# A two-layer mixture-of-experts block: the first layer's experts half dense and half sorted by expert through memory, with the order laid out anew

## The chip, the cores and the metric

The program runs on one core of a Trainium2 chip. The time is the device time of one launch in microseconds; a result is the median of several runs. The core has a matrix engine (PE), a vector engine (DVE), an activation engine (ACT), a general engine (POOL, GpSimd) and a queue engine (SP) that here only issues transfers. Each runs its own list of instructions in order; they meet through counting semaphores. PE writes only to eight accumulation banks (`bank`), which DVE and ACT empty.

## What is computed

4 batches of 512 tokens, 256 features each, go through two layers. Cut to what matters:

```
h0  = einsum('bnt,bot->bno', x, sum_g y[b,g] * weight[g] * mask) + bias        # layer 0 input
p   = softmax(h0 @ router_w.T); top 2 of 8 experts, weights normalised
x  += sum over the token's 2 experts of (h0 @ W_e + p_e) * w_e                  # 8 experts, 256 x 256
h1  = x @ W_base.T + b + 2 * sum_e w[b,e] * (x @ A_e.T) @ B_e.T                 # layer 1 input
x  += sum over 2 shared experts of swiglu(h1)                                   # F = 352 each
x  += sum over the token's 2 of 8 experts of w_e * swiglu_e(h1)
```

Every large product is made of float16 halves (high and low part) in three passes, to keep float32 accuracy.

## The kernel before

The 2048 tokens are 16 tiles of 128 rows (four per batch). `hs` holds the layer input with the feature on the partitions, `x1` the running result with the token on the partitions.

**Layer 0, dense.** All eight experts are applied to all 16 tiles. The loop `for m in range(TWO)` (PE L1100, DVE L761, ACT L538) takes two tiles at a time; inside, `j` runs over four pairs of experts. Per tile and pair PE makes six matmuls of 512 columns, and DVE adds the two experts' halves of the bank into `x1`, each with its own coefficient (zero for experts not chosen): L777, 128 instructions in all. Behind it on the same engines come, tile pair by tile pair, the turning of `x1` (`transposes`, `tr_hi`, `tr_lo`), the low-rank weights (`lora`, `wl_sum`, `wl_hi`), the layer 1 input of a batch (`layer1_input`, `h_hi`, `h_lo`), its router logits, and the token rows for the later gather (`token_rows`, `copy_rows`, bank 4 or 5 in turn). The layer 1 weights come in 16 pieces: SP loads a piece, ACT makes the high half and the scaled copy (L529, L532), POOL subtracts to the low half in eight shares (L442).

**Layer 1, shared experts.** A round `i` is a batch and one of six strips of F. PE: `gate_up(i)`, twelve matmuls of 512 columns (six in every sixth round). ACT: silu (`sil`). DVE: product (`prod`). ACT: high half (`acts`). DVE: low half. `gate_up(i)` may start when `prod(i-2)` is made. Rounds 0 to 17 (`EARLY`) run ahead of the routed tiles; within them stand `down(0)` behind round 7 and `down(1)` behind round 17, 68 matmuls of 256 columns each. DVE also does the bookkeeping of the routing between rounds: the choice of two experts (after round 2), the group sizes and slots (rounds 4 and 5), one-hot rows (`hot_lanes` within the emptying of `down(0)`, `hot_tiles` in rounds 8 to 10), `slot_tokens` (12) and the table of each tile's expert (`tile_experts`, 14), which PE loads into registers before round 17.

**Layer 1, routed experts.** 39 tiles of 128 sorted entries: POOL gathers rows by an indirect transfer, PE turns and multiplies, POOL scatters the result to memory (`results`). The gate and up products of tile i, the transposes of tile i+2 and the down product of tile i-1 are interleaved (`step`).

**The tail.** Rounds 18 to 23, `down(2)`, `down(3)`; SP loads the scattered rows back (`yg`), ACT scales the first expert's rows, POOL adds them, DVE adds the second (`combine`), then DVE adds the shared part (`accumulate`) and SP stores.

## Time and profile before

| | |
|---|---|
| median of 3 runs | 379.43 us (377.74 to 380.24) |
| profiled execution, device time | 378.77 us |
| its span, first to last instruction | 377.0 us |
| PE busy | 357.7 us, 95% of the span |
| DVE busy | 238.8 us, 63% |
| ACT busy | 166.1 us, 44% |
| POOL busy | 154.2 us, 41% |
| mean granted TensorE clock | 0.994 |

A matmul row's duration is the time through the array, which overlaps with the next; the pace of a train is its length over its count. Idle time of an engine is put down to whatever released it last.

### The profile page before, as it was taken

The page shows a single profiled execution, that of the slowest core. Times are in us where ns is not written, and L with a number is a line of the kernel's source. Part 1 is how long each engine was busy: PE and PEld are TensorE (multiplying, and loading weights), DVE is VectorE, ACT ScalarE, POOL GpSimd, SP SyncE. Part 2 cuts the span into 40 slices and gives each one's busy share as a digit, 9 for nine tenths or more (in the row PEclk, how much of TensorE's full clock was granted, in tenths as well). Part 3 has the DMA queues.
Part 4 walks back from the last instruction along what each step waited for, and adds up shares of the span by engine and source line. Part 5 has one row for each costly group of instructions (what it writes and reads, how often), then busy time and mean ns, then how long its engine had stood idle before and what let it go on. Part 6 is the DMA issues. An engine that isn't in the chain of part 4 may idle for free.

```text
span 377.0 us, 7974 instructions
## 1 busy us (share of the span) xinstructions
PE 357.7 (95%) x2713; PEld 225.4 (60%) x2714; DVE 238.8 (63%) x594; ACT 166.1 (44%) x286; POOL 154.2 (41%) x241
## 2 busy tenths in 40 slices
PE   7998999999999999989999999999999999999992
PEld 3543544455454454555447677777777777776561
DVE  1357999676766646778775455565555565546476
ACT  1045376567555765543442333333333333323560
POOL 3000564665647532000020365565665555532642
PEclk9999999999999999999999999999999999999997
DMA  7985113433443420100000122222222222212942
GB/s 217 377 330 203 54 53 119 150 92 122 141 151 128 136 69 0 58 0 2 0 28 2 44 86 84 70 84 78 75 83 80 73 78 78 80 42 74 353 161 111
DMA packets 18038, 39.26 MB, mean 104 GB/s; under 512 B 2976, under 2 KB 9376, under 8 KB 17888
## 3 DMA queue, kind: packets, MB, share of 16 engines
q1 hardware_dynamic: 13552, 28.71, 22.8%
q0 software_dynamic: 3744, 10.23, 8.7%
q8 instruction: 14, 0.23, 0.3%
q10 hardware_dynamic: 720, 0.02, 0.1%
q14 instruction: 8, 0.07, 0.1%
HBM read 29.65 MB, written 9.31 MB: 103 GB/s over the span
## 4 chain that ended last, share of the span: by engine, by line
PE 72%; DVE 16%; DMA 4%; ACT 3%; issue 3%; SPq 0%; DVEq 0%
PE bank L1000 58%; PE bank L1147 4%; PE bank L1245 3%; DVE prod L904 2%; PE bank L1016 2%; PE bank L1229 2%; ACT acts L582 2%; DVE x L892 2%; DMA w1s<-results 2%; DVE x L777 2%; DVE acts L910 1%; DMA x<-wc 1%; PE bank L1076 1%; DMA results<-yb,row_out 1%; ACT sil L572 1%
## 5 line engine op out<-in xcount | busy, mean ns | idle before, releaser
L442 POOL TENSOR_TENSOR w1s<-piece,w1s 128x170 f16<-128x170 f32 x128 | 61.6, 521 | 78.2 <-ACT piece L532 78.2
L1000 PE MATMUL bank<-w0s,hs 128*128 128x512 f16 x384 | 86.0, 379 | 1.2 <-DVE x L777 1.2
L1000 PE MATMUL bank<-w1s,rT 128*128 x468 | 76.2, 313 | 1.6 <-DVE rT L964 1.6
L451 POOL DMA_INDIRECT rows<-token_store,row_in x39 | 37.9, 971 | 86.1 <-DVE row_in L874 47.5
L777 DVE SCALAR_TENSOR_TENSOR x<-bank,coef,x 128x256 f32<-128x256 f32 x128 | 54.8, 478 | 19.4 <-PE bank L1000 19.1
L1000 PEld LDWEIGHTS bank<-w0s,hs 128*128 128x128 f16 x384 | 36.9, 98 | 43.8 <-DVE x L777 1.9
L1000 PE MATMUL bank<-hs,w1s 128*128 128x512 f16 x264 | 59.6, 379 | 2.1 <-DVE prod L904 2.1
L1000 PEld LDWEIGHTS bank<-w1s,rT 128*128 128x128 f16 x468 | 44.0, 98 | 22.1 <-issue 2.1
L456 POOL DMA_INDIRECT results<-yb,row_out x39 | 38.5, 987 | 37.1 <-ACT yb L606 37.1
L1000 PE MATMUL bank<-w1s,aT 128*128 (+1 forms) x351 | 44.8, 273 | 0.8 <-DVE aT L957 0.8
L600 ACT ACTIVATE ract<-prod 128x352 f16<-128x352 f32 x39 | 19.4, 497 | 58.5 <-DVE prod L970 33.6
L1000 PEld LDWEIGHTS bank<-hs,w1s 128*128 128x128 f16 x264 | 25.0, 98 | 32.3 <-DVE prod L904 5.2
L964 DVE COPY rT<-bank 128x256 f32<-128x256 f32 x39 | 16.6, 425 | 33.3 <-PE bank L1229 33.3
L1000 PEld LDWEIGHTS bank<-w1s,aT 128*128 128x128 f16 (+1 forms) x351 | 32.7, 98 | 4.5 <-issue 0.9
L973 DVE TENSOR_TENSOR ract<-prod,ract 128x352 f16<-128x352 f32 x39 | 20.5, 526 | 21.9 <-issue 18.5
L1147 PE MATMUL bank<-w1s,acts 128*128 128x256 f16 x272 | 30.5, 273 | 1.5 <-DVE slot_lo L839 1.2
L595 ACT ACTIVATE sil<-bank 128x352 f32<-128x352 f32 x39 | 18.1, 463 | 28.5 <-PE bank L1000 28.5
L1147 PEld LDWEIGHTS bank<-w1s,acts 128*128 128x128 f16 x272 | 26.4, 98 | 6.1 <-issue 1.7
L582 ACT ACTIVATE acts<-prod 128x512 f16<-128x512 f32 (+1 forms) x24 | 15.1, 629 | 30.7 <-DVE prod L904 30.7
L529 ACT ACTIVATE w1s<-piece 128x1360 f16<-128x1360 f32 x16 | 21.3, 1329 | 14.7 <-DMA piece<-w 14.7
L910 DVE TENSOR_TENSOR acts<-prod,acts 128x512 f16<-128x512 f32 (+1 forms) x24 | 16.7, 697 | 16.0 <-ACT acts L582 16.0
L532 ACT ACTIVATE piece<-piece 128x1360 f32<-128x1360 f32 x16 | 21.4, 1338 | 0.5
(149 smaller groups left out, 405.5 us busy)
## 6 DMA issues: line engine op xcount, KB each, us to landing
piece<-w SPq DMA_DIRECT2D x16, 680.0 KB, 3.9
w1s<-results SPq DMA_DIRECT2D x6, 512.0 KB, 8.3
x<-wc SPq DMA_DIRECT2D x4, 512.0 KB, 7.0
w1s<-xT SPq DMA_DIRECT2D x4, 512.0 KB, 11.0
w1s<-w SPq DMA_DIRECT2D x4, 512.0 KB, 10.1
token_store<-xrow SPq DMA_DIRECT2D x4, 512.0 KB, 3.3
out<-x SPq DMA_DIRECT2D x8, 256.0 KB, 2.2
x<-x SPq DMA_DIRECT2D x1, 1536.0 KB, 11.7
```

Of the source, the lines that this page charges most:

```text
L442: ins = nc.gpsimd.tensor_tensor(w1s[:, LO, at], piece[:, i % 2, part], w1s[:, HI, at], ALU.subtract)
L451: pool.indirect_dma_start(rows[:, i % 2], None, token_store, bass.IndirectOffsetOnAxis(row_in[:, i:i + 1], 0)).then_inc(s_row[i % 2], 16)
L456: pool.indirect_dma_start(results, bass.IndirectOffsetOnAxis(row_out[:, i:i + 1], 0), yb[:, i % 2], None).then_inc(s_put[i % 2], 16)
L529: nc.scalar.activation(w1s[:, HI, i * PIECE:(i + 1) * PIECE], piece[:, i % 2], ACT.Copy, scale=SW).then_inc(sm["s_pchi"], 1)
L532: nc.scalar.activation(piece[:, i % 2], piece[:, i % 2], ACT.Copy, scale=SW).then_inc(sm["s_pcsc"], 1)
L582: nc.scalar.activation(acts[0:M, c % 2, f, HI], prod[0:M, p], ACT.Copy).then_inc(sm["s_ahi"], 1)
L600: nc.scalar.activation(ract[:, q, HI], prod[:, q, 0:F], ACT.Copy).then_inc(sm["s_rhi"], 1)
L777: nc.vector.scalar_tensor_tensor(x1[:, t], bank[(n + a) % 4][:, h * D:(h + 1) * D], coef[:, t, e:e + 1], x1[:, t], ALU.mult, ALU.add).then ...
L910: nc.vector.tensor_tensor(low, prod[0:M, p], acts[0:M, c % 2, f, HI], ALU.subtract).then_inc(sm["s_alo"], 1)
L973: nc.vector.tensor_tensor(ract[:, q, LO], prod[:, q, 0:F], ract[:, q, HI], ALU.subtract).then_inc(sm["s_rlo"], 1)
L1000: mm = nc.tensor.matmul(out_ap, l, r, start=(i == 0), stop=(i == len(terms) - 1))
L1147: mm = nc.tensor.matmul(bank[4 + q][:, 0:D], acts[:, c % 2, f, a, q * P:(q + 1) * P], w_dn(b, f), start=(f == 0 and n == 0), stop=(f == ST ...
```

## The change

Layer 0's experts stay dense for the first 8 tiles (batches 0 and 1). For the other 8 (`NTR`, batches 2 and 3) every token's two entries are sorted by expert into 23 tiles of 128 slots (`TILES0`):

- POOL scatters each token row to its two slots in memory (`place`, 16 indirect transfers); the slots were set to zero before (`clear`). SP loads the 23 slot tiles (`load_rows0`, four deep), PE turns each (`operand_rows`, 4 transposes), DVE copies it to `rT0` (`operand0`), PE multiplies it with its one expert (`sorted_tile`, 6 matmuls of 256 columns), ACT empties the bank (`out0`), SP stores it (`keep_out0`), POOL gathers both entries of each token (`take`, 16 indirect transfers), and DVE adds them with their weights (`combine0`, 32 instructions).
- This needs its own choice, ranks and slots before (`selected`, `ranks(rank0, ...)`, `slots0`, `parts0`, `tile_experts0`) and token rows of layer 0's input (`rows_of_layer0`, 32 transposes; `copy_rows0`).
- The tiles stand in bursts of four behind the rounds 2 to 7 of the shared experts.
- `EARLY` is 21 instead of 18. `down(0)` and `down(1)` stand both behind round 11, in halves, between the turning of the four late tile pairs and the layer 1 input of batches 2 and 3. The bookkeeping of layer 1's routing moves to rounds 9 and 12 to 19.
- Weight pieces are converted in another sequence (`ORDER`); the last six come behind the sorted tiles, since `w0s`, the slot rows and the gathered rows lie in the same memory.

The core of the diff:

```diff
-    EARLY = 3 * ST
-    DOWN = {ST + 1: 0, EARLY - 1: 1, EARLY + 1: 2}
+    EARLY = 3 * ST + 3
+    DOWN = {EARLY + 1: 2}
-    SCALED = {EARLY + 1: (0, 1), EARLY + 3: (2,), B * ST - 1: (3,)}
+    SCALED = {EARLY + 1: (0, 1), B * ST - 1: (2, 3)}
...
@@ POOL
+            for n in range(4):
+                low_parts(n)
+            pool.wait_ge(sm["s_slots0"], 1)
+            pool.wait_ge(sm["s_zero"], 16 * 2)
+            for t in range(NTR):
+                for k in range(K_TOP):
+                    place(t, k)
+                    i = t * K_TOP + k
+                    low_part(4 + i // SHARES, i % SHARES)
...
@@ ACT
                 if m == 1:
+                    copy_rows0(range(NTD, NTD + TPB))
                     act.wait_ge(s_x1[1], 16)
                     act.wait_ge(sm["s_r0"], 2)
...
+                if i in (8, 10):
+                    piece_hi(FREE - 4 + i // 2)
+                if i in (9, 11):
+                    piece_scaled(FREE - 4 + i // 2)
+                if i == 10:
+                    exps(2, DENSE, 1.0 / (SH1 * SW))
...
@@ DVE
+                if i == 9:
+                    dve.wait_ge(sm["s_m0"], TILES0)
+                    take_logits(1, 0, DENSE)
+                    largest(DENSE)
+                    second(DENSE)
+                    selected(DENSE, "s_sel")
+                if i == 11:
+                    combine0(8)
+                    tr_lo(4)
+                    accumulate(0, (), (0, 1))
+                    combine0(10)
...
@@ PE
-            for m in range(TWO):
+            for m in range(TWO_D):
...
+                    if m == 1:
+                        rows_of_layer0(range(NTD + 2 * j, NTD + 2 * j + 2))
...
+                for t in burst(i):
+                    sorted_tile(t, places0[t % BURST])
+                    if t + 2 < TILES0:
+                        operand_rows(t + 2)
+                if i == 11:
+                    transposes(4)
+                    down(0, quarters=(0, 1))
+                    transposes(5)
+                    down(0, quarters=(2, 3))
+                    layer1_input(2)
+                    transposes(6)
+                    down(1, quarters=(0, 1))
+                    transposes(7)
+                    down(1, quarters=(2, 3))
+                    layer1_input(3)
```

`transposes(4)` waits for `combine0(8)`:

```diff
+                else:
+                    pe.wait_ge(sm["s_cmb0"], (m - TWO_D + 1) * 2 * K_TOP)
+                    pe.wait_ge(sm["s_prod"], ND * ST - 1 + (m - TWO_D) // 2)
```

How the order moves. PE before, from the turning of the token rows of the last batch to the first expert table (`ident,hs` are token rows, `hs,w1s` of 12 a round's gate and up, `w1s,acts` a down, `wls,yg` the inverse of the sorting):

```order
L1087 MATMUL bank<-ident,hs 128x128 x8
L1174 MATMUL bank<-sel,before 128x128
L1176 MATMUL bank<-sel,ones 128x128 x15
L1179 MATMUL bank<-sel,ones 128x8 x16
L1000 MATMUL bank<-hs,w1s 128x512 x30
L1147 MATMUL bank<-w1s,acts 128x256 x68
```

PE of the change, rounds 10 and 11 (one train of 18) and what stands behind them (`ident,x` turns a tile pair of `x1`, `xrow,wls` is the layer 1 input of a batch):

```order
L1286 MATMUL bank<-hs,w1s 128x512 x18
L1365 MATMUL bank<-ident,x 128x128 x4
L1470 MATMUL bank<-w1s,acts 128x256 x34
L1365 MATMUL bank<-ident,x 128x128 x4
L1470 MATMUL bank<-w1s,acts 128x256 x34
L1286 MATMUL bank<-xrow,wls 128x512 x12
L1365 MATMUL bank<-ident,x 128x128 x4
L1470 MATMUL bank<-w1s,acts 128x256 x34
L1365 MATMUL bank<-ident,x 128x128 x4
L1470 MATMUL bank<-w1s,acts 128x256 x34
L1286 MATMUL bank<-xrow,wls 128x512 x12
L1286 MATMUL bank<-hs,w1s 128x512 x12
```

Before, a whole down stood behind seven rounds with bookkeeping; now both downs stand ahead of round 12, cut in halves, each half behind a turning of tiles.

ACT of the change from round 10 to the first late tile pair (the two table loads stand around the exponential; `w1s<-piece` and `piece<-piece` are a weight piece, `xrow<-bank` the turned tile pair):

```order
L740 ACTIVATE sil<-bank 128x512
L752 ACTIVATE acts<-prod 128x512
L674 ACTIVATE w1s<-piece 128x1360
L642 ACT_TABLE_LOAD
L642 ACTIVATE ex<-ex 128x64
L642 ACT_TABLE_LOAD
L740 ACTIVATE sil<-bank 64x512
L752 ACTIVATE acts<-prod 64x512
L679 ACTIVATE piece<-piece 128x1360
L660 ACTIVATE xrow<-bank 128x2x256
```

The silu of round 11 stands behind a piece's high half and the exponential with its tables.

DVE before, from the slots behind round 5 to the first quarter of `down(0)` (`yg<-lane` are the one-hot rows, eight at a time; `x<-bank,x` empties a quarter of `down(0)`):

```order
L839 SCALAR_TENSOR_TENSOR slot_lo<-slot_hi,st 128x32
L904 SCALAR_TENSOR_TENSOR prod<-bank,sil 128x512
L910 TENSOR_TENSOR acts<-prod,acts 128x512
L904 SCALAR_TENSOR_TENSOR prod<-bank,sil 128x512
L910 TENSOR_TENSOR acts<-prod,acts 128x512
L848 TENSOR_SCALAR yg<-lane,slot_lo 128x128 x8
L922 SCALAR_TENSOR_TENSOR x<-bank,x 128x256
```

DVE of the change, rounds 15 to 18 (the slots stand ahead of it, in round 14):

```order
L1055 TENSOR_SCALAR yg<-lane,slot_lo 128x128 x16
L1115 SCALAR_TENSOR_TENSOR prod<-bank,sil 128x512
L1123 TENSOR_TENSOR acts<-prod,acts 128x512
L1055 TENSOR_SCALAR yg<-lane,slot_lo 128x128 x16
L1115 SCALAR_TENSOR_TENSOR prod<-bank,sil 64x512
L1123 TENSOR_TENSOR acts<-prod,acts 64x512
L1061 TENSOR_TENSOR wls<-tile,slot_hi 128x32x39
L1064 TENSOR_SCALAR wls<-wls,lane 128x32x39
L1066 TENSOR_TENSOR wls<-wls,order 128x32x39
L1115 SCALAR_TENSOR_TENSOR prod<-bank,sil 128x512
```

The one-hot work stands between rounds now, with no down on PE beside it.

## Rows read from the trace of the kernel before

**Rows 1.** The page, busy time of each engine over the span.

```profile
PE 357.7 (95%) x2713; PEld 225.4 (60%) x2714; DVE 238.8 (63%) x594; ACT 166.1 (44%) x286; POOL 154.2 (41%) x241
```

**Rows 2.** The chain that ended last: start us, us, what (x matmuls).

```profile
91.08 12.95 PE bank L1000 x60
...
164.92 7.58 PE bank L1147 x68
```

**Rows 3.** The timeline, PE: start us, us, line, operation, count.

```profile
150.65 0.61 PE L1087 MATMUL bank<-ident,hs 128*128 128x128 f16 x8
151.09 2.75 PE L1000 MATMUL bank<-hs,w1s 128*128 128x512 f16 x12
```

**Rows 4.** The timeline, round 2 of the shared experts: silu, product, low half.

```profile
147.65 0.60 ACT L572 ACTIVATE sil<-bank 128x512 f32<-128x512 f32 x1 [1.39 <-PE bank L1000]
...
148.28 0.69 DVE L904 SCALAR_TENSOR_TENSOR prod<-bank,sil 128x512 f32<-128x512 f32 x1 [0.95 <-ACT sil L572]
...
149.67 0.69 DVE L910 TENSOR_TENSOR acts<-prod,acts 128x512 f16<-128x512 f32 x1 [0.70 <-ACT acts L582]
```

**Rows 5.** Busy time by window, DVE: window, its length, busy us (count with edges), clock, DMA.

```profile
56.51:59.41 2.90, 2.56 (x11) 1.00 0.53 169
150.28:154.92 4.64, 4.19 (x17) 1.00 0.00 0
162.32:164.77 2.45, 2.17 (x9) 1.00 0.00 0
168.79:170.18 1.39, 1.39 (x10) 1.00 0.00 0
177.76:179.21 1.45, 1.45 (x2) 1.00 0.00 0
181.24:181.81 0.57, 0.57 (x3) 1.00 0.00 0
194.67:196.48 1.81, 1.67 (x10) 1.00 0.26 72
```

**Rows 6.** The same for ACT: the exponential between its two table loads.

```profile
168.17:171.07 2.90, 2.87 (x3) 1.00 0.00 0
```

**Rows 7.** The page, costliest groups: busy us, mean ns of one, idle before.

```profile
L777 DVE SCALAR_TENSOR_TENSOR x<-bank,coef,x 128x256 f32<-128x256 f32 x128 | 54.8, 478 | 19.4 <-PE bank L1000 19.1
L456 POOL DMA_INDIRECT results<-yb,row_out x39 | 38.5, 987 | 37.1 <-ACT yb L606 37.1
L532 ACT ACTIVATE piece<-piece 128x1360 f32<-128x1360 f32 x16 | 21.4, 1338 | 0.5
```

**Rows 8.** The timeline around the second tile pair, and a copy of two token-row tiles.

```profile
51.91 7.94 PE L1000 MATMUL bank<-w0s,hs 128*128 128x512 f16 x36 [0.61 <-DVE x L777]
...
54.44 0.63 ACT L536 ACTIVATE wls<-wl 128x512 f16<-128x512 f32 x1 [0.73 <-DVE wl L749]
...
81.63 1.09 ACT L524 ACTIVATE xrow<-bank 128x512 f16<-128x512 f16 x2
```

**Rows 9.** The timeline, PE's first matmuls of the routed tiles.

```profile
207.17 1.96 PE L1000 MATMUL bank<-w1s,rT 128*128 x12 [0.71 <-DVE rT L964]
```

**Rows 10.** Transfers: a 128 KB load by SP, KB and us to landing.

```profile
la<-lora_a SPq DMA_DIRECT2D x1, 128.0 KB, 2.0
```

**Rows 11.** The timeline of the tail.

```profile
351.16 1.71 ACT L619 ACTIVATE yg<-yg,st 128x256 f32<-128x256 f32 x4 [4.13 <-DMA yg<-results]
...
354.18 1.71 ACT L619 ACTIVATE w1s<-w1s,st 128x256 f32<-128x256 f32 x4 [1.31 <-DMA w1s<-results]
...
366.31 1.69 ACT L619 ACTIVATE w1s<-w1s,st 128x256 f32<-128x256 f32 x4
...
372.21 1.42 DVE L922 SCALAR_TENSOR_TENSOR x<-bank,x 128x256 f32<-128x256 f32 x4
```

**Rows 12.** Windows of all engines at the end: PE busy, then granted clock.

```profile
370.00:372.00 2.00, 0.00 (x0) 0.00 (x0) 2.00 (x5) 0.00 (x0) 0.31 (x1) 1.00 0.48 181
372.00:374.00 2.00, 0.00 (x0) 0.00 (x0) 1.59 (x5) 0.00 (x0) 0.00 (x0) 0.56 0.19 73
```

More of the change, by code:

```diff
@@ L284, in build_program @@
         s_row = [sem(f"s_row{c}") for c in range(2)]
+        s_load0 = [sem(f"s_load0{c}") for c in range(DEEP)]
+        s_kept0 = [sem(f"s_kept0{c}") for c in range(DEEP)]
+        s_top = [sem(f"s_top{c}") for c in range(NTR)]
         s_put = [sem(f"s_put{c}") for c in range(2)]
@@ L445, in _ @@
+            for t in range(TPB):
+                take(t)
+            low_parts(FREE)
+            for t in range(TPB, NTR):
+                take(t)
+            for n in range(FREE + 1, NP):
+                low_parts(n)
+            pool.wait_ge(sm["s_pclo"], NP)
             pool.wait_ge(sm["s_tok"], 16 * B)
@@ L906, in shared_dve @@
                 if i == 1:
-                    h_lo(1, B - 1)
+                    h_lo(1, 1)
+                for t in turned_rows(i)[first:last]:
+                    operand0(t)
                 dve.wait_ge(sm["s_ahi"], i + 1)
@@ new lines, in sorted_tile, with experts0 @@
+            def sorted_tile(i, expert_at):
+                pe.wait_ge(sm["s_x0"], i + 1)
+                if i >= 2:
+                    pe.wait_ge(sm["s_y0"], i - 1)
+                group(bank[6 + i % 2][:, D:2 * D],
+                      [(rT0[:, i % 2, a, k], w1s[:, b, bass.ds(expert_at + (W0 + k * E * D), D)])
+                       for k in range(KT) for a, b in PASSES], "s_m0")
+            def experts0(ap):
+                return nc.values_load_multi_w_load_instructions(
+                    ap, engines=(nc.tensor.engine,), min_val=0, max_val=(E - 1) * D,
+                    skip_runtime_bounds_check_because="the table's entries are clamped where it is made")[1]
```

586 lines of the change are left out of this document (419 added, 167 removed).

## The prediction

> **What bounds the kernel now.** I read the busy times first: PE works 357.7 of 377.0 us [rows 1], so its idle time is 19.3 us in all, and a change must either take work from PE or make it wait. The chain in order of time then gives PE's pace: 60 matmuls of 512 columns in 12.95 us, 0.216 each; 68 of 256 columns in 7.58, 0.112 each [rows 2]. Eight transposes and the next train start 0.44 us apart, 0.055 each [rows 3]. A round of shared experts (12 matmuls, 2.59 us) covers the path behind it: silu starts at 147.65 and the low half ends at 150.36, 2.7 us later, DVE alone is held from 148.28 to 150.36, 2.1 us [rows 4]. PE may run one round ahead of a product, not more; DVE work between two rounds that is longer than about half a us delays PE unless a down (7.6 us) stands there. That is the reading on which all of this rests: PE is full because its long trains stand beside DVE's bookkeeping.
>
> **What the change does to PE's work.** Removed: 8 tiles x 4 pairs x 6 matmuls of 512 columns, 192 x 0.216 = 41.5 us. Added: 23 x 6 = 138 matmuls of 256 columns, 15.4 us; 92 transposes of slot rows, 5.1; 32 transposes of token rows, 1.8; the extra ranks, about 0.5. Net -18.7 us. DVE loses 64 additions of 0.43 us (54.8 over 128, [rows 7]) and gets 32 plus 23 copies; it isn't the bound by sum, but by place. The rest of the sum is waits.
>
> **Waits, in PE's order.**
> *Tile pair 1 (m = 1), +6.2.* Behind expert pair 1 stand token rows 10 and 11, which wait for ACT's copies of 8 and 9; ACT makes these behind the low-rank weights at 54.44 to 55.07 [rows 8], then 0.54 a tile. So pair 2 starts at about 56.6 instead of 51.91. Two tiles further on, rows 14 and 15 wait for copies that stand behind `add_bias`, which needs `shares0`, 2.9 us of DVE [rows 5]. Following both I get the end of m = 3 8.5 us later, of which 2.3 is PE work.
> *Bursts, +3.* Per burst DVE has 2.1 + 4 x 0.42, ACT four small copies and half a piece; PE has 2.6 + 4 x 0.9. Hidden. A slot tile's load is issued only behind the store before it in SP's list and takes 2.0 us [rows 10], which just misses the last tile of a burst: 0.5 a burst. At nothing the sum is 3 less; a whole load per burst would be 12.
> *The scatter, 0.* 16 scatters of 0.99 us [rows 7] with a 0.5 us share each end some 24 us behind the slots; the first operand is wanted some 2 us after the loads land. Cover thin, priced below.
> *`transposes(4)`, +12.4.* PE has finished round 11, while `combine0(8)` is queued on DVE behind round 11's low half, and that behind this: the selection for batches 0 and 1 behind round 9 (4.64 us for 128 columns [rows 5]; at 64 columns between 2.3 and 4.6, I take 3.8, being bound by fixed cost), product 10, then on ACT the high half 10, the piece's high half 1.3 [rows 7], the exponential with its tables 2.9 [rows 6], silu 11, then product, high and low half. From the end of `gate_up(9)`: 2.9 (path of round 9) + 3.8 + 0.7 + 0.7 + 1.3 + 2.9 + 2.7 + 1.7 (four additions) = 16.7, less 0.4 of rows turned and 3.9 of PE for rounds 10 and 11: 12.4. Late next: all that follows on PE.
> *Inside round 11's block, +7.8.* `transposes(5)` and `(7)` wait for the emptying of the last quarter and four additions, 2.2 each; `transposes(6)` waits for `h_hi`, `h_lo` of batch 2 and four additions, 3.4.
> *Rounds 12 to 20, +23.9.* From `gate_up(12)`: first product at 3.4; DVE then has six rounds of 2.1, the selection 3.8, groups about 1.4 (seven tiny operations at the pace of the table's ten in 1.81), slots 2.45, 32 one-hot rows at 1.39 per eight, 5.6, and the hot tiles, two of 1.45 and one of 0.57, 3.5 with gaps [rows 5]; 29.3. ACT holds it up twice more: the copies and piece ahead of silu 14 (2.3) and the second exponential ahead of silu 16 (1.5). `s_hot` at 36.5. Then inverse 1.2, `gate_up(19)` 2.6, its path 2.8, `tile_experts` 1.8, for PE now waits for the table right behind the round that precedes it; `gate_up(20)` 2.6 with its register load 0.4; its path 2.9 and one copy 0.4: first routed matmul at 51.4. PE's work in it: 102 x 0.216 + 1.2 logits + 1.8 rows + 1.3 ranks + 1.2 inverse = 27.5.
> *Gone, -5.5.* Before, from 151.09 [rows 3] to 207.17 [rows 9], 56.1 us, PE works 150 x 0.216 + 15.2 (two downs) + 0.4 + 1.3 + 1.2 = 50.6; the rest was waits of the same kind.
> *The tail, +1.6.* Three rounds, 36 matmuls, 7.8 us, move ahead of the routed tiles. The tail isn't PE's then: ACT scaled the last rows at 366.31 because they stood behind round 23; the loads landed 3.0 us apart (351.16, 354.18), so the fourth is in by about 361 [rows 11]. POOL and DVE follow to about 366, `accumulate` starts 6.2 earlier than at 372.21. 7.8 - 6.2 = 1.6.
>
> **Sum** against the span of 377.0: -18.7 + 6.2 + 3 + 12.4 + 7.8 + 23.9 - 5.5 + 1.6 = +30.7, span 407.7. Outside the span lie 1.8 us (378.77 - 377.0), and the median of the runs is 0.7 above the profiled run: 410.2. For the clock (below) I add 1: **411 us**.
>
> The exponential's tables, weighed: both loads and the exponential took 2.90 us, with ACT busy for 2.87 [rows 6]. The Trainium skill, "ScalarE: Activation LUTs", What ACT_TABLE_LOAD costs, gives 1283 ns for a load, which is what fits into these 2.90, and about 1.4 us of drain with every switch, which doesn't. By the page each exponential would hold ACT 2.7 us longer, both on the path here: 416; by the row nothing is added.
>
> **Rivals.**
> *PE stays full.* If DVE's and ACT's paths are covered after all, what is left of the sum is -18.7 - 5.5 + 1.6 = -22.6, with 2.5 outside the profiled span's own time (1.8 and 0.7): 357. The point where it decides is `transposes(4)`: it needs the takes and the 12.4 to vanish. For it speaks only that PE was full in every stretch before; against it, DVE's own list puts round 11 ahead of the additions. 0.05.
> *Waits half as long.* Of the waits added (53.3 us) half come: 377.0 - 18.7 + 26.7 - 5.5 + 1.6, with 2.5 outside 383.6. It would need the selection and small operations far cheaper at 64 columns, and the stall of m = 1 absent. With three quarters of them, 397. 0.12 for all of these, 0.04 of it within 1% of now.
> *Memory is late.* The 2 us of cover before the first burst fails, or the gathers are late: placements of 1.5 instead of 0.99 give 8 us on the scatter, 6 past cover: 417. For it: POOL has both the transfers and the piece shares, in one list. Against: POOL idles half the time [rows 1]. 0.12.
> *The clock.* PE's granted clock was 1.00 in 370 to 372, PE idle, and 0.56 in 372 to 374 [rows 12]: between its two levels (2.4 and 1.2 GHz). After the gaps of 12, 5, 7, 5 and 3 us PE would come back at 1.2 GHz. [...] The Trainium skill, "TensorE: Matmul & The Clock Gate", HAM oscillation, says that a matmul engine which waits in between falls to half rate again and again; the rows at the end agree, and no row shows the way back up. I take 1, since most of the trains behind gaps have slack to DVE. 0.13.
> *The waits come as computed*, 400 to 415: 0.58.
>
> **Chances and range.** 1% of 379.4 is about what a measurement of this kernel can tell from no change. Faster 0.05 (PE full), same 0.04, slower 0.91 (the rest of the half-wait case, memory, clock and the main one). Below 393 lie the first rival and about two thirds of the second, 0.13; above 424 some 0.07, memory or clock on top of everything else: range 393 to 424.
>
> **What would show it.** PE busy near 339 of a span near 408. PE idle right behind round 11 for 10 to 14 us, released by DVE's `combine0`; DVE idle there behind ACT's silu. Rounds 15 to 19 with PE below 0.6 busy and DVE above 0.85. 5 us idle ahead of `gate_up(20)`, released by `te`. The 39 routed tiles unchanged. The step from the last routed tile to the end 29 instead of 35. If the gap at `transposes(4)` is below 5 us, the argument from DVE's list is wrong, and with it most of this.

## The result and the profile after

| | before | after |
|---|---|---|
| median | 379.36 us (377.74 to 380.24, 4 runs) | 451.57 us (447.39 to 455.96, 4 runs) |
| profiled execution, span | 377.0 us | 445.6 us |
| mean granted clock | 0.994 | 0.925 |

One of the four executions after, 455.96, was in a slower state of the chip; the other three have a median of 449.8 us, and the ratio and all differences below go by them. The ratio is 1.187, 95% interval 1.176 to 1.198. I had said 411, 393 to 424: the direction was right, the size was not.

The page after, busy times, for [rows 1]:

```profile
PE 357.4 (80%) x2799; PEld 232.6 (52%) x2800; DVE 244.0 (55%) x605; ACT 181.1 (41%) x320; POOL 190.5 (43%) x274
```

PE is idle for 88 us instead of 19. Its busy time did not fall to the 339 that I named: trains at half rate fill most of that up, some 16 us by the excess of their durations. From 235.5 to 262.2, rounds 15 to 18 and the inverse, PE is 0.55 busy and DVE 0.82, against the "below 0.6" and "above 0.85" of the prediction. The timeline of PE after, at the places that the prediction names (start us, us, line, operation, count, idle before and who ended it):

```profile
56.88 4.99 PE L1286 MATMUL bank<-w1s,hs 128*128 128x512 f16 x12
...
68.19 4.44 PE L1286 MATMUL bank<-w1s,hs 128*128 128x512 f16 x12
...
103.49 1.09 PE L1402 MATMUL bank<-ident,hs 128*128 128x128 f16 x8 [6.07 <-ACT xrow L665]
...
115.90 4.45 PE L1286 MATMUL bank<-xrow,wls 128*128 128x512 f16 x12 [3.37 <-DVE xrow L939]
...
123.38 0.61 PE L1503 MATMUL bank<-ident,w1s 128*128 128x128 f16 x8
...
138.06 0.40 PE L1503 MATMUL bank<-ident,w1s 128*128 128x128 f16 x4 [2.71 <-DMA w1s<-slot_rows]
...
191.12 1.12 PE L1365 MATMUL bank<-ident,x 128*128 128x128 f32 x4 [15.98 <-DVE x L1037]
192.03 5.09 PE L1470 MATMUL bank<-w1s,acts 128*128 128x256 f16 x34
...
222.59 2.75 PE L1286 MATMUL bank<-hs,w1s 128*128 128x512 f16 x12
...
250.26 5.30 PE L1286 MATMUL bank<-hs,w1s 128*128 128x512 f16 x12 [5.59 <-DVE prod L1115]
260.11 2.26 PE L1526 MATMUL bank<-wls,yg 128*128 128x78 f16 x32 [4.55 <-DVE wls L1066]
...
270.40 4.03 PE L1286 MATMUL bank<-hs,w1s 128*128 128x512 f16 x12 [5.17 <-DVE te L1092]
...
277.65 1.96 PE L1286 MATMUL bank<-w1s,rT 128*128 x12 [3.00 <-DVE rT L1250]
```

The waits that I forecast stand there, under the names that I gave. A train of 12 that takes 2.75 in [rows 3] takes 4.0 to 5.3 behind the gaps ahead of it. That is "half rate" below: the granted clock of the stretch is 0.50, 1.2 GHz, instead of 1.00, 2.4 GHz. But not every gap does it. Windows over the first and the third half of a down on PE, busy times of PE, PEld, DVE, ACT and POOL, then clock, DMA share and GB/s:

```profile
191.00:194.00 3.00, 2.88 (x14) 2.27 (x15) 0.76 (x2) 1.72 (x2) 2.98 (x6) 0.50 0.31 93
209.30:213.60 4.30, 4.27 (x38) 3.71 (x38) 1.12 (x2) 0.60 (x1) 0.00 (x0) 1.00 0.00 0
```

The second stands behind a gap of 3.15 us. New are the two waits at 103 and 116. Cut at these rows, the spans add up as follows. The forecast of each stretch is its own PE work and the waits of the sum. Bursts: 54 matmuls at 0.216, 23 tiles at 0.89, 3 of waits. Rounds 8 to 11: 42 matmuls and 16 transposes. Block: two downs, 24 matmuls and 16 transposes in float32 (0.11 each), 22.1, plus 7.8. The start of the bursts is what then remains of 407.7. The last column is an experiment, told below.

| stretch, us | forecast | after | e15_left_out |
|---|---|---|---|
| to the first operand rows | 105.1 | 123.4 | 115.3 |
| bursts, to the last sorted tile | 35.2 | 41.8 | 36.7 |
| rest of rounds 8 to 11 | 10.0 | 9.9 | 10.0 |
| wait ahead of `transposes(4)` | 12.4 | 16.0 | 15.4 |
| block behind round 11 | 29.9 | 31.5 | 34.3 |
| round 12 to the first routed matmul | 51.4 | 55.1 | 55.3 |
| routed tiles | 134.7 | 134.6 | 134.8 |
| tail | 29.0 | 33.3 | 33.8 |
| span | 407.7 | 445.6 | 435.6 |

Of the 38 us that the forecast is short, 18 lie ahead of the bursts and 7 in them.

**Who is late at 103 us.** ACT after, the same columns:

```profile
97.66 1.34 ACT L674 ACTIVATE w1s<-piece 128x1360 f16<-128x1360 f32 x1 [8.75 <-DMA piece<-w]
...
102.86 1.06 ACT L665 ACTIVATE xrow<-bank 128x512 f16<-128x512 f16 x2
...
111.93 1.34 ACT L674 ACTIVATE w1s<-piece 128x1360 f16<-128x1360 f32 x1 [6.71 <-DMA piece<-w]
```

ACT's copies of the token rows stand behind the split of weight piece 6, and that waited 8.75 us for the load. SP may load piece 6 only when the low half of piece 4 is done (`s_pclo`), and POOL makes piece 4's eight shares one by one between the scatters. Piece 7 waits for piece 5 in the same way.

**Who is late at 191 us.** DVE, then ACT:

```profile
177.34 0.62 DVE L896 TENSOR_TENSOR t<-oh 128x64 f32<-128x64 f32 x1
177.99 3.32 DVE L901 CAST sel<-t 128x64 f16<-128x64 f32 x1
181.22 0.68 DVE L1115 SCALAR_TENSOR_TENSOR prod<-bank,sil 128x512 f32<-128x512 f32 x1
...
183.81 1.28 ACT L642 ACT_TABLE_LOAD   x1
185.10 0.26 ACT L642 ACTIVATE ex<-ex 128x64 f32<-128x64 f32 x1
185.37 1.28 ACT L740 ACT_TABLE_LOAD   x1
186.67 0.59 ACT L740 ACTIVATE sil<-bank 64x512 f32<-64x512 f32 x1
...
189.39 1.67 DVE L1037 SCALAR_TENSOR_TENSOR x<-yg,part,x 128x256 f32<-128x256 f32 x4
```

This is the chain that I forecast, in its order, with one step too many: a cast that took 3.32 us. POOL at that time:

```profile
177.96 3.75 POOL L545 TENSOR_TENSOR w1s<-piece,w1s 128x170 f16<-128x170 f32 x8
```

### The profile page after: what moved, and what is told of

It is laid out like the page before. It is cut to its first block, busy times and chain, and to the rows that moved or that the text cites. A ratio compares the mean times of both kernels' runs of the same rounds, so it can differ in the third digit from the quotient of the medians.

```text
span 445.6 us, 8449 instructions
## 1 busy us (share of the span) xinstructions
PE 357.4 (80%) x2799; PEld 232.6 (52%) x2800; DVE 244.0 (55%) x605; ACT 181.1 (41%) x320; POOL 190.5 (43%) x274
## 4 chain that ended last, share of the span: by engine, by line
PE 54%; DVE 17%; DMA 8%; ACT 7%; POOL 6%; issue 5%; SPq 1%; DVEq 0%; ACTq 0%
PE bank L1286 41%; POOL slot_rows L555 4%; PE bank L1470 4%; PE bank L1610 3%; DMA w1s<-slot_rows 3%; PE bank L1302 2%; DMA piece<-w 2%; PE bank L1594 2%; DVE x L1099 2%; POOL w1s L545 2%; DVE prod L1115 2%; DMA w1s<-results 2%; DVE x L1037 2%; ACT acts L752 1%; DVE x L1158 1%
## 5 line engine op out<-in xcount | busy, mean ns | idle before, releaser
L545 POOL TENSOR_TENSOR w1s<-piece,w1s 128x170 f16<-128x170 f32 x128 | 65.4, 542 | 138.1 <-ACT piece L679 137.6
L1286 PE MATMUL bank<-w1s,rT 128*128 x606 | 95.1, 304 | 6.2 <-DVE rT L1250 3.9
L1286 PE MATMUL bank<-hs,w1s 128*128 128x512 f16 x264 | 66.9, 406 | 13.7 <-DVE prod L1115 7.5
L1286 PEld LDWEIGHTS bank<-w1s,rT 128*128 128x128 f16 x606 | 56.4, 98 | 30.2 <-issue 7.8
L1286 PEld LDWEIGHTS bank<-hs,w1s 128*128 128x128 f16 x264 | 26.4, 104 | 46.0 <-issue 13.7
L1286 PE MATMUL bank<-w1s,hs 128*128 128x512 f16 x192 | 47.2, 403 | 0.0
L1115 DVE SCALAR_TENSOR_TENSOR prod<-bank,sil 128x512 f32<-128x512 f32 (+1 forms) x24 | 16.5, 687 | 37.1 <-ACT sil L740 37.1
L1250 DVE COPY rT<-bank 128x256 f32<-128x256 f32 x39 | 16.6, 425 | 33.3 <-PE bank L1594 33.3
L1158 DVE SCALAR_TENSOR_TENSOR x<-bank,coef,x 128x256 f32<-128x256 f32 x64 | 26.7, 475 | 11.2 <-PE bank L1286 11.1
L1286 PEld LDWEIGHTS bank<-w1s,hs 128*128 128x128 f16 x192 | 19.3, 103 | 23.3 <-issue 5.0
L792 ACT ACTIVATE sil<-bank 128x352 f32<-128x352 f32 x39 | 18.1, 464 | 24.2 <-PE bank L1286 24.2
L740 ACT ACTIVATE sil<-bank 128x512 f32<-128x512 f32 (+1 forms) x24 | 14.3, 595 | 28.9 <-PE bank L1286 28.7
```

Of the source, the lines that this page charges most:

```text
L545: ins = nc.gpsimd.tensor_tensor(w1s[:, LO, at], piece[:, n % 2, part], w1s[:, HI, at], ALU.subtract)
L792: nc.scalar.activation(sil[:, q, 0:F], bank[2 * q][:, 0:F], ACT.Silu, scale=1.0 / (SH1 * SW)).then_inc(sm["s_rsil"], 1)
L1115: nc.vector.scalar_tensor_tensor(prod[0:M, p], up, SA / (SH1 * SW), sil[0:M, p], ALU.mult, ALU.mult).then_inc(sm["s_prod"], 1)
L1158: nc.vector.scalar_tensor_tensor(x1[:, t], bank[(n + a) % 4][:, h * D:(h + 1) * D], coef[:, t, e:e + 1], x1[:, t], ALU.mult, ALU.add).then ...
L1286: mm = nc.tensor.matmul(out_ap, l, r, start=(i == 0), stop=(i == len(terms) - 1))
```

## The experiments

All are edits of the changed kernel; differences are against its 449.8 us (the expectations, written beforehand, reckon from 451.6), and the kernel before, run beside each, stayed at 379.3 to 379.6. The interval of the changed kernel's ratio is 4 us to either side, and single executions lie up to 2% apart. So a time that is less than some 4 us lower shows no gain by itself, and such runs, like those with one execution, are read by their stretches.

### e1_pieces, e12_burst16, e13_shift: pieces out of the scatters

```diff
-            for n in range(4):
+            for n in range(5):
                 low_parts(n)
...
                     place(t, k)
-                    i = t * K_TOP + k
-                    low_part(4 + i // SHARES, i % SHARES)
+                if t == 1:
+                    low_parts(5)
```

> Same work as the changed kernel, another order on GpSimd: the low parts of weight piece 4 stand whole ahead of the 16 scatters, those of piece 5 whole behind the first four scatters, and the last twelve scatters follow without low parts between them. Queue theory: the operand rows of the first sorted tile come late (at 123.4 us, 105.6 forecast) largely because piece 6 cannot be loaded before piece 4's eight shares, which lie between the scatters. Then ScalarE's wait on piece 6 (8.75 us before its split of that piece) goes or falls under 2 us, TensorE's 6.1 us wait in the token rows of m = 3 and most of the 3.4 us wait ahead of the layer-1 input of batch 1 go with it, and the time falls by 7 to 12 us, ratio to the changed kernel 0.973 to 0.985. Rival, the scatters themselves or VectorE's chain hold this stretch: the split of piece 6 comes early, but TensorE waits for VectorE or for the placed rows in its place, and the time stays within 3 us.

449.38 us (446.1 to 451.92), 0.4 less, which is none. The wait for piece 6 went. In its place PE stood still without waiting for anything:

```profile
99.23 0.38 PE L1402 MATMUL bank<-ident,hs 128*128 128x128 f16 x4 [1.11 <-issue]
...
102.09 0.59 PE L1286 MATMUL bank<-hs,w1s 128*128 128x512 f16 x2 [0.97 <-issue]
104.22 1.01 PE L1286 MATMUL bank<-hs,w1s 128*128 128x512 f16 x2 [1.54 <-issue]
106.34 0.59 PE L1286 MATMUL bank<-hs,w1s 128*128 128x512 f16 x1 [1.11 <-issue]
```

Six matmuls that take 1.46 us elsewhere take 6 us, and the operand rows start at 120.2. Neither theory had this. e12 leaves piece 5 out too (`low_parts(5)` behind all scatters):

> Same work as the changed kernel; the low parts of piece 4 stand ahead of the scatters, all sixteen scatters follow each other with nothing between, and pieces 5 and on come behind. If scatters back to back starve TensorE, gaps of issue stand in its trains while they run (some 80 to 100 us), several us in sum, as in e1_pieces. If the gaps of e1_pieces were its place in the program (near 98 us), TensorE has none here between 80 and 95 us; if they were one disturbed execution, none at all.

One execution, 454.56 us. The gaps are there again, 97.0 to 103.4 us (the longest 1.91), though scatters ran back to back from 80.5. So scatters back to back don't suffice; the place in the program has a part, or the time. e13 makes PE's program longer ahead of it:

```diff
                     if m == 1:
+                        if j == 3:
+                            pe.wait_ge(sm["s_wlf"], 2)
+                            for _ in range(40):
+                                nc.tensor.matmul(bank[7][:, D:D + E], ones16[:], ones16[:, 0:E], start=True,
+                                                 stop=True)
                         rows_of_layer0(range(NTD + 2 * j, NTD + 2 * j + 2))
```

> e12_burst16 with 40 matmuls of 8 columns, that nobody reads, on TensorE inside its wait ahead of the last rows of m = 1 (near 66 us), so that its program from there on is 80 instructions longer and nothing else moves. In e12_burst16 and e1_pieces TensorE's gaps of issue began 3 matmuls into the logits (97.7 us) and 2 matmuls into the token rows behind them (99.2 us), and ended some 2 us behind the last scatter. If TensorE runs out of fetched instructions there and the fetch is what the scatters hold up, the gaps begin some 60 to 100 instructions earlier in the program, in the expert products ahead of the logits, before 96 us. If the gaps come at a time, whatever stands there, they begin again at 97 to 99 us. If neither, there are none.

One execution, 452.16 us: no such gap at all. PE passes this stretch at full pace and waits 9.84 us for piece 7's chain instead (`layer1_input(1)` at 110.94). The 40 matmuls also filled a wait, so that PE reached the logits at 94.27 instead of 96.98 and the last scatter ended at 98.7 instead of 101.1: the program's length isn't the only thing that moved. The cause of the gaps stays open. That the scatters hold up PE's supply of instructions is a guess that no run shows: by it a gap should have moved, and it went. An unlucky pair of executions isn't excluded.

### e5_spread, e11_noscatter: what the scatters cost

e5 is e1 with the last twelve scatters spaced by the shares of piece 6:

```diff
+                    if i == 3:
+                        low_parts(5)
+                    if i > 3 and i % 3:
+                        low_part(6, (i - 4) // 3 * 2 + (i - 4) % 3)
```

> Same work as the changed kernel. As in e1_pieces the low parts of piece 4 stand ahead of the scatters and those of piece 5 behind the first four, but the last twelve scatters are spaced again, by the eight shares of piece 6. In e1_pieces TensorE lost some 7 us between 97.9 and 107.8 us in gaps that wait for nothing, two matmuls in 2 us, while scatters followed each other every 1.27 us; in the changed kernel, with 1.70 us between them, there were no such gaps. Crowding theory: scatters back to back starve the other engines of something they share, and spacing ends that: no gaps of issue, gate_up(0) starts at 99 to 101 us instead of 104.4, operand rows at 114 to 117 instead of 123.4, time 6 to 9 us below the changed kernel. Rival, the gaps are there whenever TensorE reaches this stretch early, spacing or not: operand rows again at 119 to 121, time 0 to 4 us below.

446.48 us (444.93 to 447.03), 3.3 less. PE:

```profile
97.21 0.61 PE L1405 MATMUL bank<-ident,hs 128*128 128x128 f16 x8
97.66 1.46 PE L1289 MATMUL bank<-hs,w1s 128*128 128x512 f16 x6
...
112.78 1.03 PE L1506 MATMUL bank<-ident,w1s 128*128 128x128 f16 x8 [3.42 <-DMA w1s<-slot_rows]
```

No wait and no gap up to 109 us; then PE waits for the scattered rows themselves, and the operand rows start 10.6 us earlier. At the last sorted tile 7.2 are left, at the first routed matmul 1.6: the block ran more of its trains at half rate (`transposes(4)` to `gate_up(12)` grew). e11 leaves the scatters out:

```diff
-                    place(t, k)
-            sp.wait_ge(sm["s_placed"], 16 * K_TOP * NTR)
```

> The changed kernel without its sixteen scatters and without SyncE's wait for them; the low parts of pieces 4 and 5 stand where they stood. The sorted tiles read zeros, so the first layer's output of batches 2 and 3 and all behind it differ; the amount of work stays but for the tokens' experts in the second layer, whose tiles are as many. It prices the scatters: I took them as free. If they hold up the weight pieces as e5_spread suggests, operand rows come at 108 to 112 us instead of 123.4, and the time is 8 to 14 us below the changed kernel; if the scatters are covered and the spacing alone mattered, 0 to 4 us below.

437.47 us (436.98 to 439.4), 12.3 less, inside what was expected. The operand rows start at 110.14:

```profile
109.53 0.75 PE L1284 MATMUL bank<-rs,hs 128*128 128x8 f16 x24
110.14 0.61 PE L1501 MATMUL bank<-ident,w1s 128*128 128x128 f16 x8
```

From 68.6 us, where the second wait of m = 1 ends, up to there PE has no wait of a microsecond. So 110.1 is PE's own pace here and 13.3 of the 18.3 us belong to the scatters and what queues behind them. The other 5.0 are mostly the two trains of m = 1 at half rate, 4.99 and 4.44 instead of 2.75 each: 3.9.

### e6_sp: the stores out of the loads' way

```diff
-                keep_out0(i)
+                if i >= 2:
+                    keep_out0(i - 2)
```

> Same work; on SyncE the store of sorted tile i's output stands two tiles later, behind the load of tile i + 6's rows, so that a load never waits behind a store that waits for ScalarE. Theory: the bursts took 41.6 us instead of 34.7 because loads stand behind stores; then the waits on the slot rows' DMA (0.40, 2.71, 0.17 and 0.30 us) go or halve and the bursts take 38 to 39.5 us. Rival: a load lands late because it takes 2.8 to 3.0 us with other transfers under way, or because its buffer comes free late; then the 2.7 us wait stays at over 2 us and the bursts at 41 to 42.

447.98 us, one execution. No wait for `slot_rows` above 1 us is left, and the bursts run from 123.3 to 159.8, 36.5 instead of 41.8. PE at the end of them:

```profile
158.97 0.83 PE L1289 MATMUL bank<-w1s,rT 128*128 x6 [1.69 <-DVE rT L1027]
...
185.76 1.12 PE L1368 MATMUL bank<-ident,x 128*128 128x128 f32 x4 [16.00 <-DVE x L1040]
```

Shorter than the low end of the 38 to 39.5 expected. The same edit gives 36.8 to 39.3 in the four runs below that hold it, and every execution without it took 41.8 to 45.4: the store ahead of each load is shown as the cause. The loads themselves are not quicker in e6, 2.8 us as before.

### e3_te, e4_exps: two forecast waits

```diff
                 if i == 18:
+                    tile_experts()
                     slot_tokens()
-                if i == 19:
-                    tile_experts()
```

> Same work; VectorE works out the table of experts of the routed tiles in round 18 ahead of the slot tokens instead of in round 19 behind them. Theory: the table is free of the inverse, and VectorE waits for the inverse there, so the table costs nothing and round 20's wait for it (5.2 us in the changed kernel) goes: round 12 to the first routed matmul falls from 55.1 to 50 to 51.5 us. Rival: VectorE's own chain of rounds 18 and 19 is the bound, the inverse's wait on VectorE grows by the table's time, and the stretch stays at 54 to 55 us.

The wait is gone: from the inverse to the first routed matmul 12.2 us (269.55 to 281.73) instead of 17.5 (260.11 to 277.65). But the table then stood between the inverse and the slot tokens, not inside the wait for it as I had put it. Time 452.89, one execution with a clock of 0.907.

```diff
-                if i == 10:
-                    exps(2, DENSE, 1.0 / (SH1 * SW))
                 if i == 15:
+                    exps(2, DENSE, 1.0 / (SH1 * SW))
```

> Same work; ScalarE's exponential of the dense half, with its two table loads, stands in round 15 beside that of the sorted half instead of in round 10. Theory: it stands in the chain that ends the wait behind round 11 (piece, tables and exponential 183.81 to 186.65, then silu of round 11), so that wait of 16.0 us falls by 2.5 to 3 us, and since the two exponentials now share their table loads, nothing is paid later: 2.5 to 3.5 us less in all. Rival: VectorE's selection is late enough that ScalarE waits for it anyway, and the wait falls by under 1 us.

The wait is 13.14 us instead of 15.98, 2.8 less. The time, 455.85 us in one execution with a clock of 0.903, does not show it.

### e7_block, e8_lock: behind round 11

```diff
                 if i == 11:
+                    down(0)
                     transposes(4)
-                    down(0, quarters=(0, 1))
                     transposes(5)
-                    down(0, quarters=(2, 3))
```

(with DVE's list to match, the selection at the block's end, and e4's edit)

> Same work, another order behind round 11: the whole down product of batch 0 stands ahead of the transposes of tiles 8 to 11, VectorE adds the sorted experts' results of the first four tiles before it takes in that product, the dense half's selection stands behind the last low part of the block instead of behind round 9 (only its copy of the logits stays), and the exponential stands in round 15. Order theory: of the 16.0 us ahead of the transposes and the 7.3 us of waits in the block most is order, not data. Then the down product starts at about 180, the transposes follow at about 188, and round 12 starts 9 to 12 us earlier than 222.6; the selection's 5 us are found again in rounds 12 to 20 in part, and the time is 5 to 11 us below the changed kernel. Data theory: the rows gathered back from memory end last, the transposes wait for them wherever they stand; round 12 starts under 5 us earlier, the time moves by less than 4 us.

445.57 us (444.46 to 447.07), 4.2 less. The down starts at 176.5 and `transposes(4)` at 187.6, and round 12 starts at 217.95 instead of 222.59, from a last sorted tile 1.5 us later: 6.2 us for three edits at once, of which the exponential's move was worth 2.8 in e4. That lies between the two theories (under 5, 9 to 12) and decides for neither. What it met next was ACT:

```profile
181.82 1.34 ACT L674 ACTIVATE w1s<-piece 128x1360 f16<-128x1360 f32 x1 [3.63 <-DMA piece<-w]
183.19 0.59 ACT L740 ACTIVATE sil<-bank 64x512 f32<-64x512 f32 x1
```

A weight piece's load holds silu 11, right behind the chain that was taken away.

```diff
-            low_parts(FREE)
             for t in range(TPB, NTR):
                 take(t)
+            low_parts(FREE)
```

> Same work; on GpSimd the eight low parts of piece 10 stand behind all sixteen gathers instead of between the first eight and the last eight. In the changed kernel VectorE's cast of the selection (128x64 to 16 bits) took 3.32 us instead of 0.23 while those eight parts ran. Port theory: GpSimd's two-input operations hold VectorE's cast off; then the cast takes 0.2 to 0.3 us here, VectorE's selection ends some 3 us earlier and the wait ahead of the transposes falls by 2 to 3.5 us, unless the later piece holds ScalarE up in its place. Rival, the cast is slow for another reason (a semaphore, its position): it stays over 2 us.

DVE and PE:

```profile
176.38 0.20 DVE L901 CAST sel<-t 128x64 f16<-128x64 f32 x1
...
186.53 1.11 PE L1365 MATMUL bank<-ident,x 128*128 128x128 f32 x4 [12.82 <-issue]
195.73 0.66 PE L1365 MATMUL bank<-ident,x 128*128 128x128 f32 x4 [3.27 <-DVE x L1037]
```

The cast takes 0.20 us, the selection is short again (3.7 us from the copy of the logits to the cast's end, where it was 7.2), the wait is 3.2 less. The low parts then fell on the second group of additions, whose wait is 3.27 instead of 2.10. 449.72 us, one execution.

### e2_fill: the clock alone

```diff
+            def fill(n, b):
+                for _ in range(n):
+                    nc.tensor.matmul(b[:, D:2 * D].rearrange("p (a n) -> p a n", a=2), ones16[:],
+                                     ones16[:].unsqueeze(1).to_broadcast([P, 2, P]), start=True, stop=True)
...
                 if i == 11:
+                    fill(112, bank[5])
                     transposes(4)
```

> Same work as the changed kernel plus matmuls that nobody reads (256 columns each) on TensorE ahead of seven waits: 18 before the last rows of m = 1, 42 before the token rows (2,3) of batch 0, 24 before the layer-1 input of batch 1, 112 before the transposes behind round 11, 38 before rounds 18 and 20, 32 before the inverse. At full rate 0.11 us each, so each train is shorter than the wait that it stands in. Clock theory: the trains at half rate behind long waits cost time of their own (by the excess of their durations some 16 us, 8.7 of it before the bursts). Then the granted clock is 0.97 or more instead of 0.925, the half of the down products behind round 11 takes some 2.6 us instead of 5.1, and the time falls by 8 to 16 us. Rival, the waits are set by VectorE, ScalarE and GpSimd, and the slow trains only fill what would be waited for anyway: the clock rises, the waits grow by as much as the trains shrink, and the time moves by less than 4 us.

448.88 us (445.46 to 449.24), 0.9 less, which is none, at a clock of 0.962. The operand rows start at 120.6, 2.8 earlier; behind them nothing is gained: `transposes(4)` at 191.38, first routed matmul at 278.2. PE:

```profile
179.85 8.46 PE L1422 MATMUL bank<-ones 128*128 128x256 f16 x76 [1.00 <-issue]
191.38 1.12 PE L1365 MATMUL bank<-ident,x 128*128 128x128 f32 x4 [3.07 <-issue]
192.29 5.02 PE L1479 MATMUL bank<-w1s,acts 128*128 128x256 f16 x34
```

The filling ended at 188.3, PE was idle for 3.07 us, and the next train ran at half rate as before (5.02 against 5.09). Round 18's train did shrink, from 5.30 to 2.76, and the inverse behind it came no earlier, 37.5 us after round 12 in both. But the inverse and round 19 were not reached by the filling:

```profile
260.30 2.26 PE L1535 MATMUL bank<-wls,yg 128*128 128x78 f16 x32 [3.60 <-DVE wls L1066]
262.36 4.70 PE L1286 MATMUL bank<-hs,w1s 128*128 128x512 f16 x12
```

So the clock theory holds ahead of the bursts, the rival for round 18, and what full rate is worth in the block and behind the inverse e2 doesn't show.

### e9_all, e10_all_fill, e14_late_low: do the gains add up?

e9 is e5, e6, e7 and e3 together.

> Same work as the changed kernel, with four of the edits above together: the scatters spaced as in e5_spread, SyncE's stores two tiles later (e6_sp), the order behind round 11 of e7_block, the table of experts in round 18 (e3_te). One by one they moved their own places by 10.6 us (operand rows earlier), 5.3 us (bursts shorter), 4.6 us (round 12 earlier, less the 0.9 us that its bursts began earlier) and 5.2 us (no wait in round 20), while the whole time moved by 4 to 6 us only. Additive theory: the places are in series and their gains stay where nothing behind them gives them back: 451.6 less some 24 us, 424 to 431. Clock theory: what is gained ahead of the block behind round 11 is paid back by longer trains at half rate in the block and in rounds 12 to 20 (in e6_sp that part took 4.8 us more than in the changed kernel): 432 to 440.

424.06 us (422.72 to 427.63), 25.8 less. What adds up is the gains at their places, 10.6 + 5.3 + 4.6 + 5.2 = 25.7. The totals alone had not shown it: e5 and e7 lay 3.3 and 4.2 us lower, e6 1.8 in one execution, and e3 no lower in one.

e10 puts filling into its waits:

```diff
+                    fill(16, bank[3])
                     transposes(4)
                     transposes(5)
+                    fill(12, bank[3])
                     layer1_input(2)
+                    fill(38, bank[3])
                     transposes(6)
```

> As e9_all, plus matmuls that nobody reads on TensorE ahead of its waits: 18 in m = 1, 20 ahead of the first operand rows, 16 ahead of the transposes behind the down product, 12 ahead of the layer-1 input of batch 2, 38 and 12 ahead of the next two transposes, 12 and 38 ahead of rounds 17 and 18, 32 ahead of the inverse. If trains at half rate are what gives the gains back, the clock rises to 0.97 or more and the time lies 5 to 12 us below e9_all. If the waits are set by VectorE and ScalarE whatever TensorE's rate, it stays within 3 us of e9_all.

419.42 us (417.84 to 421.77), clock 0.966, another 4.6 less: just under what the clock theory asked. DVE and POOL in it:

```profile
180.02 4.50 DVE L1042 SCALAR_TENSOR_TENSOR x<-w1s,part,x 128x256 f32<-128x256 f32 x1
180.02 5.94 DVE L1042 SCALAR_TENSOR_TENSOR x<-w1s,part,x 128x256 f32<-128x256 f32 x4
...
177.23 7.66 POOL L548 TENSOR_TENSOR w1s<-piece,w1s 128x170 f16<-128x170 f32 x16
```

The first of the four additions alone took 4.50 us (the two DVE rows are the same instructions, over a shorter and a longer window); the train of low parts ended at 184.9.

```diff
+            pool.wait_ge(sm["s_cmb0"], K_TOP * NTR)
             for n in range(FREE + 1, NP):
                 low_parts(n)
```

> As e10_all_fill, but GpSimd begins the low parts of pieces 11 and on only when VectorE has added all the sorted experts' results. In e10_all_fill four of VectorE's additions (128x256 each, 0.41 us elsewhere) took 5.94 us at 180.0 while sixteen low parts ran from 177.2 to 184.9, and the transposes of tiles 12 and 13 waited 4.7 us behind 38 matmuls of filling for them. Port theory: VectorE is held off by GpSimd's two-input operations; the four additions then take 1.6 to 2 us, that wait falls under 1.5 us and the time by 3 to 5 us, less what the later pieces cost in rounds 12 to 20 (they have no reader before the routed tiles). Rival: the additions wait for gathered rows that land late; they end at the same time, and the time stays within 1.5 us of e10_all_fill.

413.37 us (412.12 to 415.43), ratio 1.091 (1.087 to 1.096) to the kernel before, another 6.0 less, more than the 3 to 5 expected. DVE and POOL:

```profile
179.85 1.66 DVE L1043 SCALAR_TENSOR_TENSOR x<-w1s,part,x 128x256 f32<-128x256 f32 x4
...
188.84 7.54 POOL L548 TENSOR_TENSOR w1s<-piece,w1s 128x170 f16<-128x170 f32 x16 [10.29 <-DVE x L1043]
```

The same additions at the same place: 1.66 us. It wasn't the gathered rows. This is the fastest version found, and it stays 34 us above the kernel before.

### e15_left_out: only what the sum did not hold

The edits of e5, e6, e8, e14 and e2 together.

> The changed kernel with only those faults taken out that my sum of 407.7 us did not hold, and every wait left that it did hold (the order behind round 11, the exponential in round 10, the table of experts in round 19 stay): the pieces' low parts and the scatters as in e5_spread, SyncE's stores two tiles later, GpSimd's low parts out of the way of the selection (e8_lock) and of the sorted results' additions (e14_late_low), and the matmuls of e2_fill ahead of seven waits. If these are what the sum lacked, the time comes near it: 451.6 less 7 (operand rows earlier, by what is left of it behind the bursts), 5 (bursts), 3 (selection), 2 (additions) and 5 (clock) is 429, and what then stays above 411 is terms that were sized too small (block, rounds 12 to 20, tail: by the trace of the changed kernel 1.6, 3.7 and 4.3 us, and 3 of clock). If they act on each other or the gains are covered, it stays above 437.

435.97 us (433.82 to 438.19), 13.8 less, 7 above the 429 expected. The table above has its stretches. Three reasons stand in its trace. The filling ahead of the token rows and the layer 1 input, 4.6 and 2.6 us, now stood where no wait was left; in e5 the rows were there at 112.8, so 2.5 of the 115.3 is filling. And the selection, short again, only uncovered ACT's wait for a piece, 1.33 us at 168.03, and additions of 2.42 instead of 1.67. The wait ahead of `transposes(4)` fell by 0.6 only. And in the block, where the 112 matmuls of filling had again ended 3 us too early, two halves of a down ran at half rate instead of one, which makes it 2.8 us longer:

```profile
178.36 6.31 PE L1486 MATMUL bank<-w1s,acts 128*128 128x256 f16 x34
...
187.67 5.09 PE L1486 MATMUL bank<-w1s,acts 128*128 128x256 f16 x34
```

## Why the prediction was wrong, point by point

**What bounds the kernel, and what changes for PE: right.** PE was full and became idle; the routed tiles kept their 134.6 us. What failed is the sum of the waits, and in it first the term "the scatter, 0".

**"Tile pair 1, +6.2": right.** The two waits are 4.37 and 2.65, 7.0. The train that I put at 56.6 starts at 56.88. That it would run at half rate behind the wait belongs to the clock.

**"The scatter, 0": wrong, the largest error, 13.3 us.** I called the cover thin and asked when the rows would be in memory. I didn't follow what else hangs on POOL's list between the scatters: its shares free the piece buffers, SP loads the next piece on that, ACT splits the piece ahead of its row copies, PE waits for these. e11 prices the whole (110.1 instead of 123.4, 12.3 us of time), e5 the queue alone (10.6 at the operand rows); the 2.6 between them are PE waiting for the rows themselves, so the cover failed too. The rival "memory is late" put 6 us on it and looked at the scatters' duration; that was 0.99, not longer than before.

**"Bursts, +3": undersized, by 6.6.** I had seen that a load stands behind a store, and priced it at 0.5 a burst with the 2.0 us of [rows 10]. A slot load took 2.8 here (median), but that isn't the fault: it took as long in e6, which takes away 5.3 of the 6.6 by the order of the stores alone. What I had wrong is that the delay stays within a burst.

**"`transposes(4)`, +12.4": the mechanism right, the size 16.0.** Every step of the chain is in the trace. The 3.6 missing are the cast and the operation ahead of it, held off by POOL; e8 takes 3.2 away. e4 confirms the exponential's 2.9 in the chain with 2.8; the tables cost what the row said, 2.9 from 183.81 to 186.67, with no drain on top. How much of this wait the order made and how much the data stays open: e7 took back 6.2 us of the wait and the block together.

**"Inside round 11's block, +7.8": 2.10, 3.15 and 2.10, 7.35.** Most of what the block took beyond that, 31.5 instead of 29.9, is its first transposes and its first half of a down at half rate, 1.12 and 5.09 instead of 0.66 and 3.87.

**"Rounds 12 to 20, +23.9": 27.6.** The forecast waits are there, 5.2 for the table with them (e3: 5.3 less). Step by step, the inverse starts 37.5 us behind round 12 instead of 36.5; it takes 2.1 up to round 19 instead of 1.2; round 20 follows 8.2 later instead of 7.6; and from there it is 7.25 to the first routed matmul instead of 5.9, with round 20's train at 4.03 instead of 2.75. (The steps of my forecast add up to 51.2, not to the 51.4 that I wrote.) So the inverse and round 20 at half rate are some 2.2 of the 3.7, one more place where the clock was missing. The first step's 1.0 is DVE's and ACT's pace, and I didn't test which operation. With full rate in both, e10 and e14 take 11.0 from the inverse to the first routed matmul where e9 takes 12.1.

**"The tail, +1.6": 5.9.** `accumulate` starts 25.1 us behind the last routed tile; I had 24.2. The rest stands behind it: the span ends 6.8 us behind the last addition, where it was 3.4. It isn't the outputs. The DMA engines stop moving data some 2 us behind that addition in both kernels, and what is longer is a stretch in which no engine and no transfer works. In the fifteen variants the span ends 5.1 to 6.8 us behind the last addition. The cause is open.

**The clock, +1: undersized.** No row stood behind the 1; the rival on the clock had the mechanism. On PE's path the half rate measures 3.9 in the two trains of m = 1, where I had looked for none, 1.7 in the block and some 2.2 behind round 18. In time, filling is worth nothing that the runs can tell alone (e2, 0.9) and 4.6 once the other waits are out (e10 against e9). Where DVE is late anyway, as for round 18, it costs nothing.

So four of the terms (tile pair 1, `transposes(4)`, the block, rounds 12 to 20) held to within 4 us each, and what e15 takes out, 13.8 us, is the part of the 39 that I can show by time as faults missing from the sum; without its misplaced filling it would be some 16. Single edits showed 13 (scatters), 5 (stores) and 3 (cast) at their own places. The rest of the 39 is read from the trace and not tested, the 3.4 at the very end above all.

## What to carry to other kernels

When work is put between two shares of a loop on a helper engine, follow what the shares release, as far as the engine that is full: here shares, buffer, load, split, row copy, matmul. Four edits of which the best alone brought 4.2 us brought 25.8 together, so read a single edit by its stretch, not by the total. And dummy matmuls in a wait helped here only where they reached its end and nobody else was late.

## What the hardware showed that I had not expected

**DVE held by POOL, at times for the rest of a train.** A cast of 128x64 took 3.32 us instead of 0.20 (e8) beside eight low parts of 3.75 us. Four additions took 5.94 instead of 1.66 (e14) beside sixteen of 7.66, the first alone 4.50. The Trainium skill, "SBUF — State Buffer", Who interferes with whom, says that DVE and GpSimd share a port pair as an exclusive lock: a cast can need it, and an operation with two inputs in SBUF does beside a GpSimd operation that reads SBUF. The trace agrees, and shows more than a lock for one instruction would give: a low part lasts 0.47 us in the train, the cast waited 3.1. But it isn't always so. In e15 four such additions began 0.9 us before a train of low parts and took 2.42 in all, and in e14 the small two-input operations of the selection took 0.3 to 0.54 instead of 0.22 in the middle of a train. What decides between the two is not shown.

**PE standing still beside scatters**, two matmuls in 2 us (e1) with nothing to wait for, in two executions (e1, e12) out of three with scatters 1.27 us apart, and in no execution where shares stood between them. The cause is open.

**Filling that ends early is lost.** In e2 PE was busy with it up to 188.3 and then idle for 3.07 us; the next 34 matmuls took 5.02 us, where they take 3.88 at 2.4 GHz. The length of the gap doesn't decide it: in the same execution 34 matmuls took 3.88 behind an idle time of 3.15 us (209.51).
